# Sharing the expansion of the softmax weights between ScalarE and VectorE in seven steps of a cross-attention kernel

## The reference

```python
x = x + xattn(layernorm(x), ctx, ctx, Wq, bq, Wk, bk, Wv, bv, Wd, bd)   # x, ctx (32, 128, 256)
    # q, k, v = projections; reshape(B, -1, 16, 16); softmax(q k^T / 4) v; @ Wd.T + bd
x = x + ffn(layernorm(x), w_red, wg, W1, b1, W2, b2)
    # logits = (x @ w_red) @ normalised(wg).T; gates = softmax(logits); idx, score = argmax, max
    # gelu(x @ W1[idx] + b1[idx]) @ W2[idx] + b2[idx], times score
```

## Time and profile before

| | |
|---|---|
| median of 3 runs | 434.36 us (430.93 to 436.53) |
| profiled execution | 435.58 us, span 433.7 us |
| busy share of the span: TensorE, VectorE, ScalarE, GpSimd | 89%, 72%, 54%, 69% |
| steps 24 to 30, the ones that change | 177.46 to 231.08 us of the span, 53.62 us |

### The profile page before, as it was taken

One profiled execution on the slowest core, in us unless ns is written; L12 is line 12 of the kernel. 1 busy time (PEld: TensorE's weight loads), 2 busy tenths in 40 slices (PEclk: granted clock), 3 DMA queues, 4 the chain that ended last, 5 costly groups with the idle time before them and its releaser, 6 DMA issues.

```text
span 433.7 us, 11372 instructions
## 1 busy us (share of the span) xinstructions
PE 384.0 (89%) x3785; PEld 306.2 (71%) x3785; DVE 312.9 (72%) x667; ACT 234.6 (54%) x781; POOL 297.8 (69%) x399
## 2 busy tenths in 40 slices
PE   3998799999999889899797587988999999999990
PEld 3776577666767667656565475777999999999970
DVE  0564899988989889999999774578465555556640
ACT  2334378868768587777562465563244444444420
POOL 1568668869779587786765965565377777777751
PEclk9699899999999999999999898999899999999996
DMA  5776668697796788966575500131012222222200
GB/s 168 228 201 200 159 186 225 204 243 197 211 242 193 203 210 229 249 187 166 160 169 164 149 27 26 50 115 50 26 63 76 74 69 66 68 66 68 66 18 0
DMA packets 97513, 59.31 MB, mean 137 GB/s; under 512 B 70446, under 2 KB 88527, under 8 KB 97456
## 3 DMA queue, kind: packets, MB, share of 16 engines
q1 hardware_dynamic: 92336, 48.44, 40.9%
q0 software_dynamic: 3744, 9.53, 7.5%
q10 hardware_dynamic: 1376, 0.61, 0.5%
HBM read 37.41 MB, written 22.07 MB: 137 GB/s over the span
## 4 chain that ended last, share of the span: by engine, by line
PE 46%; DVE 16%; DMA 14%; issue 10%; POOL 7%; SPq 3%; ACT 2%; DVEq 1%; ACTq 0%; POOLq 0%
PE bQ L1079 14%; DMA qkv_scr<-qkv 10%; PE bKV L1047 8%; PE bL L1047 6%; PE bKV L897 4%; POOL kx L368 4%; DMA ql<-qkv_scr 2%; PE bL L905 2%; DVE qkv L472 2%; PE bO L905 2%; PE bY L933 2%; PE bQ L969 2%; DMA wgT<-in_L_ffn_wg 2%; SPq L244 2%; PE bT L1061 2%
## 5 line engine op out<-in xcount | busy, mean ns | idle before, releaser
L368 POOL TENSOR_TENSOR kx<-ql,mask 128x2048 f32<-128x2048 f32 x32 | 117.9, 3683 | 40.0 <-issue 28.3
L1079 PE MATMUL bQ<-w,wA 128*128 x312 | 74.3, 381 | 3.3 <-DVE r L712 2.7
L462 DVE TENSOR_TENSOR ax<-bA,mask 128x2048 f32<-128x2048 f32 x32 | 73.3, 2290 | 0.6 <-PE bA L985 0.6
L1079 PEld LDWEIGHTS bQ<-w,wA 128*128 128x128 f32 x312 | 56.2, 190 | 10.6 <-issue 4.5
L897 PE MATMUL bKV<-wA,xcT 128*128 128x512 f32 x128 | 61.9, 607 | 1.4 <-DVE qkv L472 1.4
L391 POOL DMA_INDIRECT out<-r,isc x39 | 41.3, 1059 | 22.3 <-issue 13.4
L349 POOL TENSOR_TENSOR rs<-ve,half 128x2 f32<-128x2 f32 x39 | 28.3, 726 | 24.9 <-ACT ve L733 24.8
L414 POOL DMA_INDIRECT r<-row_scr,ig x39 | 40.5, 1038 | 6.0 <-issue 2.4
L842 ACT ACTIVATE wA<-bL,r 128x128 f32<-128x128 f32 x76 | 21.6, 367 | 41.3 <-PE bL L1047 26.6
L842 ACT ACTIVATE wA<-bKV,r 128x128 f32<-128x128 f32 x80 | 22.8, 368 | 37.6 <-PE bKV L1047 20.8
L905 PE MATMUL bO<-ax,pad 128*32 128x128 f32 x1024 | 36.2, 284 | 6.7 <-DVE ax L462 6.4
(11 more groups left out here) (200 smaller groups left out, 726.9 us busy)
## 6 DMA issues: line engine op xcount, KB each, us to landing
qkv_scr<-qkv SPq DMA_DIRECT2D x32, 384.0 KB, 3.5
ql<-qkv_scr SPq DMA_DIRECT2D x32, 384.0 KB, 4.4
row_scr<-cat SPq DMA_DIRECT2D x32, 133.5 KB, 3.5
w<-in_L_ffn_W SPq DMA_DIRECT2D x16, 256.0 KB, 4.5
xt<-in_x SPq DMA_DIRECT2D x15, 256.0 KB, 4.8
ct<-in_ctx SPq DMA_DIRECT2D x15, 256.0 KB, 5.4
w1b<-in_L_ffn_W SPq DMA_DIRECT2D x12, 256.0 KB, 4.3
w1b<-in_L_ffn_W SPq DMA_DIRECT2D x2, 512.0 KB, 7.8
```

The lines of the kernel that those rows point to most:

```text
L368: eng.tensor_tensor(block(kx[:, z % 2, :]), spread_heads(ql[z % 2][:, :, 0:HD]), mask_b, ALU.mult).then_inc(S["kx"], 1)
L462: eng.tensor_tensor(block(ax[:, :]), spread_heads(bA[:, 0:C].rearrange("p (l i) -> p l i", l=NH)), mask_b, ALU.mult).then_inc(S["ax"], 1)
L1079: i_ = eng.matmul(bQ[:, 0:C], hT[b % 2][:, k, :], w2[:, bass.ds(eb * (KH * C) + k * C, C)], start=(k == 0), stop=(k == KH - 1))
```

## The change

In steps 24 to 30 ScalarE, behind its exponential, writes the first SHARE = 3 of the 8 blocks of `ax`, each as one activation with a column of the mask as scale. VectorE waits for it and writes the other five in one instruction. Pieces 0 and 2 to 6 of the early routing, which stood behind the K and V additions, now stand ahead of the expansion; piece 1 stays where it was.

```diff
+SHARE = 3
+        def shared(s1):
+            return ROUTE <= s1 + 4 < ROUTE + 7
+
         def expand(eng, s1):
             eng.wait_ge(S["tr_a"], s1 + 1)
             if s1 > 0:
                 eng.wait_ge(S["pvo"], s1)
-            eng.tensor_tensor(block(ax[:, :]), spread_heads(bA[:, 0:C].rearrange("p (l i) -> p l i", l=NH)),
-                              mask_b, ALU.mult).then_inc(S["ax"], 1)
+            b = SHARE if shared(s1) else 0
+            if b > 0:
+                eng.wait_ge(S["ax0"], s1 + 5 - ROUTE)
+            eng.tensor_tensor(block(ax[:, :])[:, :, b:, :],
+                              bA[:, 0:C].rearrange("p (l i) -> p l i", l=NH).unsqueeze(2).broadcast_to((P, NH, NB - b, HD)),
+                              mask[:, b:].unsqueeze(1).unsqueeze(3).broadcast_to((P, NH, NB - b, HD)),
+                              ALU.mult).then_inc(S["ax"], 1)
...
+                if ROUTE <= t < ROUTE + 7 and t != ROUTE + 1:
+                    vector_early(eng, t - ROUTE)
                 if live(s1) and live(a):
                     expand(eng, s1)
                 if live(a) and t >= 4:
                     vector_kv(eng, a)
-                if ROUTE <= t < ROUTE + 7:
-                    vector_early(eng, t - ROUTE)
+                if t == ROUTE + 1:
+                    vector_early(eng, 1)
...
+                if live(s1) and shared(s1):
+                    scalar_expand(eng, s1)
                 if live(w):
                     eng.wait_ge(S["gm"], w + 1)
...
+        def scalar_expand(eng, s1):
+            eng.wait_ge(S["tr_a"], s1 + 1)
+            eng.wait_ge(S["pvo"], s1)
+            for b in range(SHARE):
+                i_ = eng.activation(block(ax[:, :])[:, :, b, :], bA[:, 0:C].rearrange("p (l i) -> p l i", l=NH), ACT.Copy,
+                                    scale=mask[:, b:b + 1])
+            i_.then_inc(S["ax0"], 1)
```

More of the change, by code:

```diff
@@ L56 @@
         "ld_b1 ld_bc ld_moe ld_b2 pad0 filled ident iotas const zeroed mask nmax gpow wrt ctr0 ctr bdm gmm gate gx gxs "
-        "wtr wT wqs wqc gsq nr2 wide tr_in xT qq kv kvad qad xb kx pad qk mx lsub exp sm rsm norm tr_a ax pvo oT wd x2 nb gm gsub "
+        "wtr wT wqs wqc gsq nr2 wide tr_in xT qq kv kvad qad xb kx pad qk mx lsub exp sm rsm norm tr_a ax0 ax pvo oT wd x2 nb gm gsub "
         "scaled score nm0 nm1 va0 va1 ve0 ve1 pw rs rsd oh cnt rv selr selp selk invmm texp idg ids ig isc yo yb "
```

## The result

The changed kernel takes 438.17 us in the median (20 runs), the kernel before 434.08 (20 runs): 4.1 us apart. The measured ratio of the two is 1.0103, 95% interval 1.008 to 1.0127, which makes 4.5 us slower (3.5 to 5.5). The forecast was 4.5 us slower, 438.9 us. Ratios leave out the few executions that were over 1.5% longer than the fastest of their kernel, and where a trace is of such a one, its total is compared with nothing.

What follows compares the result with a forecast made beforehand. VectorE was taken to set the pace. Each expansion saves 0.80 us, but held pieces and step 25's wait make the seven steps 58.1 us for 53.6: 434.36 + 4.5 = 438.9 us, range 430.4 to 442.4.

Steps and rivals of the forecast that it cites:

- what would show it: Signs expected in the changed trace: long first and second piece instructions, 1.49 us expansions, a ScalarE wait in step 25 alone.
- hold-up: In moved pieces, VectorE's two-input SBUF instructions stand still until GpSimd's kx, then xt's addition, is through; chance 0.55.
- The sum: Steps 24 to 30, where expansion starts at kx's end + piece + 0.45: together 58.1 us for 53.6, 4.5 us lost.
- G: In each step, the moment VectorE is done with the maximum of the gate logits, the old expansion's place.
- the transfer's lag: From the small copy L483 of step n-2 to the landing of kx's load in step n: 7.9 us.
- hold-up term of 0.45 us: Between kx's end and the expansion, besides the piece: xt's 0.75, less twice 0.14, less the gap between the held instructions.
- (a): Rival: only one hold-up a step, xt doesn't come in between; 2.1 us lost, 436.5 us; chance 0.20.
- (b): Rival: no hold-up, kx and two-input instructions run side by side; 3.5 us gained, 430.9 us; chance 0.15.
- (c): Rival: later stores and loads raise kx's lag from 7.9 to 9 us; 7 us lost, 441.4 us; chance 0.10.
- TensorE's idling: TensorE's wait for the expanded weights in the changed steps, costed at nothing, as VectorE has 2.7 and 3.5 us of work meanwhile.

Runs made afterwards that it cites:

- the halved kx: The changed kernel, with GpSimd's kx writing only half of its columns in the seven steps: 51.83 us for the seven, ratio 1.000 to the kernel before.
- its control: The kernel before, with the same half of kx left out in the same seven steps: 53.11 us for the seven, ratio 1.001 to the kernel before.
- second trace: The changed kernel run once more, unaltered, for another trace: seven steps 58.77 us, ratio 1.0139 to the kernel before.
- share alone: The changed kernel with all routing pieces back behind the K and V additions, ScalarE still writing three blocks: seven steps 57.43 us, ratio 1.0102 to the kernel before.
- move alone: The kernel before with pieces 0 and 2 to 6 ahead of the expansion, all eight blocks on VectorE: seven steps 62.36 us, ratio 1.0274.
- xt of one column: The changed kernel, with GpSimd's addition into xt doing one column of 264 in the seven steps: 57.15 us for the seven, ratio 1.0045 to the kernel before.
- kx behind the piece: The changed kernel, with kx of steps 24 and 26 to 30 waiting for its own step's piece: seven steps 61.42 us, ratio 1.0152 to the kernel before.

## Why the prediction was right

**The mechanism.** As the changed kernel's trace has it: held first instructions (0.72 to 1.56 us in the pieces that were moved, 0.35 in piece 4, where a reduction runs first), held second ones (0.66 to 0.77; 0.40 in piece 0, where a reduction lies between), one wait of 1.12 us in step 25 and none elsewhere, expansions of 1.49: as listed under what would show it. (A second wait, 1.71 us for the gate logits, stands ahead of piece 0 in step 24; the prediction had it in its sum.) That the hold-up is kx's is shown by the halved kx and its control. What no row of before had shown, a two-input instruction under kx itself, is now shown. The Trainium skill (SBUF — State Buffer, "Who interferes with whom") has it as a rule for exactly these pairs, and the traces agree: 1.44 us for 0.31.

**The sum.** Step for step, forecast and measured: 9.38 and 9.38, 8.40 and 8.44, 7.78 and 7.71, 7.99 and 8.06, 8.15 and 7.79, 7.96 and 7.91, 8.45 and 8.12; 58.1 and 57.4 together. The largest misses are steps 28 and 30. kx of step 28 began 2.90 us ahead of G, where I had 2.64, the transfer's lag being 7.7 instead of 7.9; kx of step 30 began 2.91 ahead, where I had 2.61. Steps 29 and 30 had kx follow ScalarE (no idle time ahead of it), where I had taken the transfer. In steps 24 and 27 the agreement is partly luck: kx ended 0.21 and 0.27 us later against G than forecast, and the hold-up term of 0.45 us was too large by nearly as much. In steps 26 to 30 it measures 0.26 to 0.43 (from kx's end to the expansion, less the piece): xt's addition too ends by its own length less 0.15 behind the instruction that put it off, which the row of L696 already had (245.04 to 245.64), and the sum took its full 0.75. The ratio says 4.5 us, 0.7 more than the seven steps of that execution, so that both it and the forecast read 4.5 is luck as well. The interval is 1.0 each way, so the 0.7 may be nothing; it may also be executions with the lower clock, whose step 24 cost 1.7 us more in the second trace. How often they occur is open. With an interval of 1.0 us each way a change of 4.5 us is clear of noise; the prediction had thought that 8.7 us was about the least that can be told.

**The parts.** Three activations take 1.18 to 1.20 us together (I took 1.14), one 0.477. ScalarE's blocks were ready 1.20 after G (1.15), the subtraction for the gate logits started at G + 0.93 or 0.94 in steps 25 to 30 (1.03), at G + 1.35 in step 24. Piece 0, which waits for that result, started at G + 1.79, not at about G + 1.35; its wait of 1.71 us was hidden under kx as argued: that piece ended its first instruction 0.18 behind kx's end at 177.99.

**The rivals.** (a), one hold-up, is excluded by the second instructions. (b), no hold-up, is excluded; the halved kx, which still left xt's and some of kx's own hold-up, gained 1.8 us in the seven steps. (c), the circle with the transfers, didn't decide: the lag was 8.0, 8.2 and 7.7 us in steps 26 to 28, and from step 29 on kx followed ScalarE.

**What the prediction didn't see.** First, the clock: I costed TensorE's idling at nothing, as it has time to spare in a step of VectorE's. It now waits 1.5 to 2.9 us for the expansion in six steps, where it waited 0.3 at most before (and 0.75 to 1.35 for the softmax, a wait that is gone in them), and in executions in which its clock then falls, the scores become the late ones. Secondly, the new wait ties VectorE to ScalarE's whole queue. I named what is queued behind the waiting expansion, and not what is queued ahead of ScalarE's blocks, where the copy into `pad` waits for a transfer. In the changed kernel this didn't show, as the pieces cover it; in the share alone it cost 1.2 us of the 3.8 by which the seven steps grew.

## What to carry to other kernels

Before moving a VectorE instruction that reads two SBUF tensors, or copies within SBUF, look at what GpSimd runs at the new place. In this kernel a 3.67 us elementwise instruction there held it for all that was left of it, and the next one in GpSimd's queue got in between once more. Work that is taken off the bounding engine is worth what it takes less the wait for the helper, and that wait is counted from the helper's queue, with all that stands ahead in it. Where the next start depends on the start two steps before, a change on one of the links shows only by half in each step, as in steps 29 and 30 here (0.28 for 0.55).

## What the runs showed that I had not expected

The gain without any hold-up is small too: three blocks take 0.80 us a step off VectorE and gave 0.20 at most in steps 26 to 30, two take 0.53 and gave 0.30, since TensorE's transposition leaves ScalarE 0.8 us until VectorE asks.

TensorE's clock fell in single steps after waits for the expansion of 1.64 us (share alone, step 25), 2.02 (move alone, step 27), 2.76 (xt of one column, step 24), 3.12 (the second trace) and 4.52 (move alone, step 24), and behind the two pairs of shorter waits in the kernel with kx behind the piece; it stayed at 1.00 after waits of 2.91 (first trace, step 24), 2.08 and 1.99 (move alone, steps 26 and 30) and 2.06 (xt of one column, step 27). So the length of the last wait alone doesn't decide. What does, these runs don't show.
